# Moving waits off the small wait-carrying products, and reordering the attention work among the convolutions, in a one-core attention and convolution kernel

## What is computed

```python
q = einsum('bhwd,de->bhwe', x, Q_P)
k = einsum('bhwkd,de->bhwke', stk, K_P)      # stk: the nine shifted views, zero padded
v = einsum('bhwkd,de->bhwke', stk, V_P)
alpha = softmax(einsum('bhwke,bhwe->bhwk', k, q) * mask, axis=-1)
t = x + einsum('bhwk,bhwke->bhwe', alpha, v)
t_in = t
t = relu(conv3x3(t, ff1) + b1)
t = relu(conv3x3(t, ff2) + b2)
t = relu(conv3x3(t, ff3) + b3)
return t_in + t
```

## Time and profile before

| | |
|---|---|
| median of 3 runs | 2383.03 us (2382.46 to 2383.31) |
| the profiled execution's own time | 2380.99 us |
| its span, first to last instruction | 2379.0 us |
| TensorE busy | 96% |
| VectorE busy | 80% |
| ScalarE busy | 47% |
| DMA engines, mean share | 46.4% |
| mean granted TensorE clock | 0.993 |

### The profile page before, as it was taken

The page is one execution under the profiler, slowest core; times in us unless marked ns, Lnnn a source line. Parts: engine busy times, 40 slices in busy tenths (PEclk is TensorE's granted clock), DMA queues, the critical chain, the costliest instruction groups (busy, mean ns, idle before and its releaser), DMA issues.

```text
span 2379.0 us, 65460 instructions
## 1 busy us (share of the span) xinstructions
PE 2287.5 (96%) x25180; PEld 1317.7 (55%) x25180; DVE 1895.5 (80%) x2851; ACT 1127.4 (47%) x3108; POOL 15.5 (1%) x24
## 2 busy tenths in 40 slices
PE   4999999999999999999999999999998999999998
PEld 2655555555565555555555555555555555555554
DVE  4888888887588888888768888888877888888886
ACT  1554455444454554454345544544535445444543
POOL 2000000000000000000000000000000000000000
PEclk9999999999899999999999999999999999999999
DMA  4444544544355445444344454445434544454443
GB/s 125 138 137 136 158 134 125 160 141 134 94 158 152 137 126 162 139 136 137 123 138 144 126 160 140 135 136 157 135 124 119 156 147 138 127 160 136 128 153 119
DMA packets 291286, 328.79 MB, mean 138 GB/s; under 512 B 89300, under 2 KB 223252, under 8 KB 284564
## 3 DMA queue, kind: packets, MB, share of 16 engines
q1 hardware_dynamic: 291164, 327.17, 46.4%
HBM read 152.50 MB, written 33.82 MB: 78 GB/s over the span
## 4 chain that ended last, share of the span: by engine, by line
PE 79%; DVE 12%; issue 5%; ACT 1%; DVEq 1%; DMA 1%; SPq 0%; ACTq 0%
PE conv_banks L476 28%; PE conv_banks L435 16%; PE conv_banks L490 15%; PE mix_bank L413 6%; PE score_banks L387 3%; DVE work L836 3%; PE score_banks L398 3%; PE mix_bank L425 3%; DVE dt L764 2%; DVE tf L746 2%; DVE dt L760 2%; PE score_banks L381 1%; PE proj_bank L420 1%; PE score_banks L395 1%; PE conv_banks L450 1%
## 5 line engine op out<-in xcount | busy, mean ns | idle before, releaser
L476 PE MATMUL conv_banks<-dodd,w3f 128*64 128x512 f32 (+1 forms) x1656 | 500.3, 579 | 6.2 <-DVE dodd L760 3.9
L476 PE MATMUL conv_banks<-deven,w3f 128*64 128x512 f32 (+1 forms) x1656 | 489.9, 566 | 0.0
L598 ACT ACTIVATE prob<-score_banks,negmax 128x100 f32<-128x100 f32 x1040 | 343.0, 343 | 273.4 <-DVE negmax L726 273.4
L435 PE MATMUL conv_banks<-dt,w1f 128*64 128x256 f32 (+3 forms) x4224 | 414.4, 384 | 0.0
L490 PE MATMUL conv_banks<-duh,w2h 64*128 64x512 f32 (+2 forms) x1632 | 362.2, 423 | 4.0 <-ACT m_sb L634 2.1
L664 ACT ACTIVATE relued<-work,bias 128x1024 f32<-128x1024 f32 (+2 forms) x136 | 150.4, 1108 | 435.7 <-DVE work L836 435.7
L490 PE MATMUL conv_banks<-duh,w2l 64*128 64x512 f32 (+2 forms) x1632 | 329.5, 382 | 0.0
L435 PEld LDWEIGHTS conv_banks<-dt,w1f 128*64 128x64 f32 (+1 forms) x4224 | 219.2, 135 | 138.6 <-issue 65.9
L490 PE MATMUL conv_banks<-dul,w2h 64*128 64x512 f32 (+2 forms) x1632 | 286.4, 383 | 0.0
L476 PEld LDWEIGHTS conv_banks<-dodd,w3f 128*64 128x64 f32 x1656 | 138.8, 137 | 226.5 <-issue 181.3
L490 PEld LDWEIGHTS conv_banks<-duh,w2h 64*128 64x128 f32 x1632 | 168.7, 185 | 137.7 <-issue 104.5
(11 more groups left out here) (97 smaller groups left out, 3224.2 us busy)
## 6 DMA issues: line engine op xcount, KB each, us to landing
xk<-x_keys SPq DMA_DIRECT2D x66, 800.0 KB
xc<-x_bands SPq DMA_DIRECT2D x66, 650.0 KB, 5.0
dodd<-dodd SPq DMA_DIRECT2D x68, 512.0 KB, 5.1
xr<-x_bands SPq DMA_DIRECT2D x264, 128.0 KB, 3.5
out<-work SPq DMA_DIRECT2D x60, 512.0 KB, 2.7
dt<-dt SPq DMA_DIRECT2D x68, 256.0 KB, 2.3
deven<-deven SPq DMA_DIRECT2D x68, 256.0 KB, 5.7
duh<-duh SPq DMA_DIRECT2D x68, 256.0 KB, 2.4
```

The source lines that it names most:

```text
L435: mm = nc.tensor.matmul(bank[(LOWER, UPPER)[o], n * 256 + lo * 64:n * 256 + hi * 64], w1f[i][rows, m, s, o * C:o * C + C], dt[rows, lo + s ...
L476: return nc.tensor.matmul(bank[rows, lo * 128:hi * 128], w3f[:, m, s, odd * C:odd * C + C], source[:, lo + s // 2:hi + s // 2, m], start=s ...
L598: last = nc.scalar.activation(prob[:, g % 2, a], score_banks[:, g % 2, a * KEYS:(a + 1) * KEYS], ACT.Exp, bias=negmax[:, g % 2, a:a + 1], ...
```

## The change

On TensorE the small products are taken out of the loop. The waits that stood before them are functions of their own (`await_band`, `await_r`, `await_prob`, `await_y`), and are called inside the stream of products that comes before (`ahead`): before the last two products of a `conv3_tile`, before the last pair of `begin2` or `end2`, or inside the first `conv1` group. The waits of `conv1` itself stay where they are. Only in the prologue do the small products stay, as `hold`.

The third convolution's streams run in the order 0, 1, 2, 3 (before 0, 2, 1, 3). `begin2` takes both row taps against the high part of the data, and `go_on2` keeps only the low part; in the four streams together the products are the same. The first `mix` moves from between `go_on2` and `begin2` to behind the last `conv3_tile`; the second `turn` moves from behind `go_on2(1)` to between `begin2(1)` and `go_on2(1)`.

On ScalarE `keep_r(b, 0)` goes to the front, `keep_r(b, 1)` ahead of `keep_u2`, and `keep_m2(CONV3)` ahead of `relu_conv1`. On VectorE part 1 of `t_inputs` moves past the step's border, to behind `outer(ODD)`; `max_scores(b, 0)` goes ahead of `middle1`, and part 1 of the `inputs` of the second convolution's results goes behind `outer1`, between the two `scale`. SyncE's order of transfers is not changed.

```diff
-    return ORDER3.index(j) if which == CONV3 else 4 + 2 * j + (which == EVEN)
+    return j if which == CONV3 else 4 + 2 * j + (which == EVEN)
...
+            def hold(bank):
+                nc.tensor.matmul(bank[:, 0:2], eye16_sb[:], window_sb[:, 0:2], start=True, stop=True)
+            def await_band(b):
+                pe.wait_ge(t_ready, b * 2)
+                pe.wait_ge(xc_in, b * 16 + 16)
+                pe.wait_ge(xs_in, b * 32 + 32)
...
             def r_product(b):
-                if not isinstance(b, int):
-                    pe.wait_ge(t_ready, b * 2)
-                pe.wait_ge(xs_in, b * 32 + 32)
-                nc.tensor.matmul(proj_bank[:, 0:2], eye_sb[LOWER], eye_sb[LOWER, 0:2], start=True, stop=True)
...
+            def await_r(b, half):
+                pe.wait_ge(r_ready, b * 2 + (half + 1))
+                if half:
+                    pe.wait_ge(probt_ready, b * 2 + 1)
             def scores(b, half):
-                pe.wait_ge(r_ready, b * 2 + (half + 1))
-                if not isinstance(b, int) or half:
-                    pe.wait_ge(probt_ready, b * 2 + half)
-                nc.tensor.matmul(score_banks[:, 0, 0:2], eye16_sb[:], window_sb[:, 0:2], start=True, stop=True)
...
+            def await_prob(b, half):
+                pe.wait_ge(prob_ready, b * GROUPS + (2 * half + 2))
             def turn(b, half):
-                pe.wait_ge(prob_ready, b * GROUPS + (2 * half + 2))
-                nc.tensor.matmul(score_banks[:, 0, 0:2], eye_sb[LOWER], eye_sb[LOWER, 0:2], start=True, stop=True)
...
+            def await_y(b):
+                pe.wait_ge(y_ready, b * 2 + 2)
             def v_product(b):
-                pe.wait_ge(y_ready, b * 2 + 2)
-                pe.wait_ge(r_ready, b * 2 + 2)
-                nc.tensor.matmul(proj_bank[:, 0:2], eye_sb[LOWER], eye_sb[LOWER, 0:2], start=True, stop=True)
...
-            def conv1(G, k, b, outer):
+            def conv1(G, k, b, outer, att=False):
-                nc.tensor.matmul(conv_banks[:, 2 * outer, 0:2], eye16_sb[:], window_sb[:, 0:2], start=True, stop=True)
                 for n, m in enumerate(streams):
                     for i in range(2):
+                        if att and n == 1 and i == 1:
+                            await_r(b, 0)
...
 -            def conv3_tile(G, k, j):
+            def conv3_tile(G, k, j, ahead=None):
...
                 tap(1, 1, False, False)
+                if ahead:
+                    ahead()
                 tap(0, 1, False, True)
                 tap(1, 3, False, True).then_inc(tile_done, 1)
...
 -            def begin2(G, k, j):
+            def begin2(G, k, j, ahead=None):
...
-                for w in (w2h, w2l):
-                    tap2(k, EVEN, j, LOWER, 0, w, duh, w is w2h, False)
-                    tap2(k, ODD, j, UPPER, 0, w, duh, w is w2h, False)
+                for s in range(2):
+                    for w in (w2h, w2l):
+                        if ahead and s == 1 and w is w2l:
+                            ahead()
+                        tap2(k, EVEN, j, LOWER, s, w, duh, s == 0 and w is w2h, False)
+                        tap2(k, ODD, j, UPPER, s, w, duh, s == 0 and w is w2h, False)
             def go_on2(G, k, j):
-                for w in (w2h, w2l):
-                    tap2(k, EVEN, j, LOWER, 1, w, duh, False, False)
-                    tap2(k, ODD, j, UPPER, 1, w, duh, False, False)
...
 -            def end2(G, k, j):
+            def end2(G, k, j, ahead=None):
...
+                    if ahead and n == 2:
+                        ahead()
...
             def step(G, k, b, att):
                 if att:
-                    pe.wait_ge(xc_in, b * 16 + 16)
                     r_product(b)
-                conv1(G, k, b, False)
+                conv1(G, k, b, False, att)
                 if att:
                     scores(b, 0)
                 conv1(G, k, b, True)
                 conv3_tile(G, k, 0)
-                conv3_tile(G, k, 2)
+                conv3_tile(G, k, 1, (lambda: await_prob(b, 0)) if att else None)
                 if att:
                     turn(b, 0)
-                conv3_tile(G, k, 1)
+                conv3_tile(G, k, 2, (lambda: await_r(b, 1)) if att else None)
                 if att:
                     scores(b, 1)
                 conv3_tile(G, k, 3)
+                if att:
+                    mix(b, 0)
                 begin2(G, k, 0)
                 go_on2(G, k, 0)
-                if att:
-                    mix(b, 0)
-                begin2(G, k, 1)
+                begin2(G, k, 1, (lambda: await_prob(b, 1)) if att else None)
+                if att:
+                    turn(b, 1)
                 go_on2(G, k, 1)
-                if att:
-                    turn(b, 1)
...
-                begin2(G, k, 2)
+                begin2(G, k, 2, (lambda: await_y(b)) if att else None)
                 if att:
                     v_product(b)
...
-                end2(G, k, 3)
+                next_band = None if k == BANDS - 2 else b if k == BANDS - 1 else b + 1
+                end2(G, k, 3, None if next_band is None else lambda: await_band(next_band))
...
         @block.scalar
...
             def step(G, k, b, par, att):
+                if att:
+                    keep_r(b, 0)
                 if k:
                     relu_conv2(G, k - 1, ODD, 1)
-                if att:
-                    keep_r(b, 0)
-                if k:
                     relu_conv2(G, k - 1, EVEN, 1)
+                if att:
+                    keep_r(b, 1)
                 keep_u2(G, k)
                 if att:
                     exps(b, 0)
                     exps(b, 1)
-                    keep_r(b, 1)
+                keep_m2(G, k, CONV3)
                 relu_conv1(G, k)
-                keep_m2(G, k, CONV3)
...
         @block.vector
...
             def step(G, k, b, par, att):
                 if k:
                     outer(G, k - 1, ODD, 1)
+                if k < BANDS:
+                    t_inputs(None, b - 1, k % 2, 1)
+                if k:
                     outer(G, k - 1, EVEN, 1)
                     inputs(G, k - 1, ODD, 0, 1)
                     inputs(G, k - 1, EVEN, 0, 1)
+                if att:
+                    max_scores(b, 0)
                 middle1(G, k)
                 if att:
-                    max_scores(b, 0)
+                    max_scores(b, 1)
+                outer1(G, k)
+                if att:
+                    scale(b, 0)
+                if k:
+                    inputs(G, k - 1, EVEN, 1, 1)
+                if att:
+                    scale(b, 1)
                 if k:
                     inputs(G, k - 1, ODD, 1, 1)
-                if att:
-                    max_scores(b, 1)
-                if k:
-                    inputs(G, k - 1, EVEN, 1, 1)
-                outer1(G, k)
-                if att:
-                    scale(b, 0)
-                    scale(b, 1)
...
                     add_x(k, b, par, 1)
                     add_x(k, b, par, 0)
-                    for part in range(2):
-                        t_inputs(G, b, par, part)
+                    t_inputs(G, b, par, 0)
```

More of the change, by code:

```diff
@@ L532, in _ @@
             pe.wait_ge(xc_in, 16)
+            pe.wait_ge(xs_in, 32)
+            hold(proj_bank)
             r_product(0)
+            await_r(0, 0)
+            hold(score_banks[:, 0])
             scores(0, 0)
+            await_prob(0, 0)
+            hold(score_banks[:, 0])
             turn(0, 0)
+            await_r(0, 1)
+            hold(score_banks[:, 0])
             scores(0, 1)
             mix(0, 0)
+            await_prob(0, 1)
+            hold(score_banks[:, 0])
             turn(0, 1)
             mix(0, 1)
+            await_y(0)
+            hold(proj_bank)
             v_product(0)
@@ L589, in _ @@
                 step(g0 + BANDS, BANDS, b0 + BANDS, True)
-            for j in ORDER3:
+            for j in range(4):
                 conv3_tile(ALL_STEPS, 0, j)
@@ L688, in step @@
             def step(G, k, b, par, att):
-                if k:
-                    relu_conv2(G, k - 1, ODD, 1)
                 if att:
@@ L870, in _ @@
             dve.wait_ge(w_ready, 3)
-            for part in range(2):
-                t_inputs(None, 0, 0, part)
+            t_inputs(None, 0, 0, 0)
             def step(G, k, b, par, att):
@@ L891, in step @@
                     scale(b, 0)
+                if k:
+                    inputs(G, k - 1, EVEN, 1, 1)
+                if att:
                     scale(b, 1)
+                if k:
+                    inputs(G, k - 1, ODD, 1, 1)
                 inputs(G, k, CONV1, 0)
```

10 lines of the change are left out of this document (4 added, 6 removed).

## The result

The changed kernel takes 2293.84 us (median of 4 runs, 2291.31 to 2295.79) against 2383.14 for the kernel before: a ratio of 0.9625, 95% interval 0.9609 to 0.9642. That is 89.3 us less; 82.8 were forecast, a median of 2300. Its profiled execution takes 2292.98 us, 2291.0 of them the span.

The account below looks back on a forecast made before the run. TensorE's stream, busy 96% of the span, was taken as the bound. Terms 0.44 + 0 + 0.22 + 0.43 + 0.19 = 1.28 us a step, 82.8 in all, gave 2298.2, as a median 2300; range 2284 to 2316.

Parts of the forecast that it names:

- the first case: Whole kernel: all moved waits are met, 2300 us, own range 2284 to 2316; chance 0.63.
- The regular step: Steps k = 2 to 14, from one `r_product` to the next: 34.68 us before, 33.40 forecast.
- `conv1` and `scores`: Four bfloat16 small products dropped on TensorE: 0.11 us each, 0.44 a step; bounds nothing and 0.18 each.
- `r_product`: Its small product behind the last `end2` pair: worth nothing, wholly covered while `conv1` waits for `outer(ODD)`.
- `turn`: Two float32 small products on LOWER only: 0.11 us each, 0.22 a step; bounds nothing and 0.31.
- `v_product`: Small product and wait for ScalarE's copy after `begin2(2)`: 0.43 us saved, bounds 0.2 and 0.49; wait met with 0.05 spare.
- The mixing: First `mix` moved behind the third convolution: one leaving and one coming back saved, 0.19 us; bounds 0 and 0.3.
- The tightest place: VectorE's `middle1` ahead of the third convolution: done at 8.0 to 8.25 us, needed by 8.37, 0 to 0.25 spare.
- The rival that `middle1` comes late: Handing over before the third convolution costs 0.5 us more, each step gives back 0.5: 2332 us; chance 0.22.
- the forecast's own signs of being wrong: A gap before the third convolution, a stall inside `begin2` or a `conv3_tile`, or longer first products of a stream.
- The part of `t_inputs`: Part 1 left ahead of `outer(ODD)` on VectorE would make that about 0.5 us late; moved, it waits for nothing.
- The rival by the floor: Skill's 25 ns floor: four small products worth 0.10 us, step gain about 0.6, near 2345; no chance of its own.

Follow-up runs that it names:

- the version with the masks in the gap: Changed kernel with the four mask products of the first `scores` moved between `r_product` and the inner `conv1`: 2282.88 us, ratio 0.9580.
- the version after it: Changed kernel with the mask products between `r_product` and inner `conv1`, and `middle1` ahead of the first `max_scores` in steps k = 0, 1 and 16: 2279.64 us.

## Why the prediction was right, point by point

**The total.** Right: 2300 forecast, 2293.8 measured, inside the first case's own range of 2284 to 2316. Two errors of opposite sign lie in it. The regular step was to be 33.40 and is 33.06; 52 of them give 1.62 x 52 = 84 us where 1.28 x 52 = 67 were counted. The twelve short steps with attention and the four without were to give 16; they and the prologue give about 4, the rest of the span's 88.0. So there is luck in the total: with the step's true 1.62 in all 64 steps, the forecast's own reckoning ends at 2381.0 - 103.7 - 0.9 + 2.0 = 2278, outside its range. That range isn't the sum of the bounds either: with the lower ones of the turns (0), the mixing (0) and the V product (0.2) together, 0.64 a step, it would have reached up to 2341.

**The short steps.** Measured from the first product of the inner `conv1` to the next one's: k = 0 is shorter by 0.9 us on average, k = 1 by 0.40 (30.98 to 30.58), k = 15 longer by 0.06 (28.22 to 28.28), and the four k = 16, the last of them to the span's end, are longer by 3.5 in all. The prologue gives 1.8 (`conv1` starts at 50.40 against 52.20). A step k = 16 takes 33.52 where the clock doesn't fall behind the wait for `middle1`, against 33.42 and 33.64 before (35.87 in the first pair); 35.20 where it falls; 37.92 in the third pair, where the turn of the loop behind it takes 6.64 us without work instead of 3.9 as well.

**`conv1` and `scores`.** Terms of 0.11 each. Shown for `conv1` and for the second `scores`; in the first `scores` 0.23, since the 128 x 128 product stood between two streams of 64 x 64 products and brought a change of shape (from the inner `conv1`'s first product to the outer one's it took 4.11 and takes 3.77, and 0.11 of the 0.34 are the outer `conv1`'s own). Mis-sized by 0.12: 0.56 for the four where 0.44 was forecast.

**`r_product`.** Costed at nothing. Shown twice: with its product put back, and with four masks more in the gap, the start of `conv1` stays at 1.81.

**`turn`.** 0.22 for two, measured 0.80 - 0.58 = 0.22 for the first (0.80 from 740.38 to 741.18 in the experiment that puts it back), and 0.17 for the second (from the turn to the second mixing 753.73 - 751.10 = 2.63 in that experiment, 728.20 - 725.74 = 2.46 without), so 0.39. The row of `r_product`'s small product, of the same kind, has 0.20 to the next start (1380.49 to 1380.69) and would have been the nearer one.

**`v_product`.** 0.43 forecast; 0.34 measured. The copy is waited for a little still: the last pair takes 0.39 where a pair and the way out take 0.33 (701.57 to 701.90). The mechanism is the one written down, 0.05 to spare turned into about 0.06 short.

**The mixing.** 0.19 forecast, 0.33 measured by putting it back: the way out of the third convolution (0.1) was missing from the term, and the mixing itself is shorter there by 0.04.

**The tightest place.** `middle1` was named as such, with 0 to 0.25 to spare; in the regular step it has about 0.15 when the handing over is counted. The order that the forecast redid holds there: `scale` 1 ended at 12.20 and part 1 of ODD at 13.34 us into the step (12.2 and 13.3 forecast). The rival that `middle1` comes late is true in the steps k = 16, whose short first convolution gives it less cover, and for 0.20 us in k = 15. There the forecast was too simple: it gave every step with attention the regular step's gain, said of `r_product` in k = 0 and k = 1 that these steps "can only add to the gain", and didn't look at k = 16. In k = 16 TensorE waited 2.08 us, and in three of the four the clock fell behind the wait. In k = 0 and k = 1 the probabilities are late in the second tile (0.31 and 1.44 us). Both are among the forecast's own signs of being wrong; they came in the short steps alone.

**The orders of ScalarE and VectorE.** The forecast used the new orders' times without saying what they are worth. Put back beside the new order of the tiles, they cost 1.1 us a step, as much as the small products. So dropping the products and moving the waits would have given little without them; how much of the 1.1 hangs on the order of the tiles wasn't measured (0.7 us would stay by the estimate above). The part of `t_inputs` gives 0.47, forecast 0.5.

**The rival by the floor.** Putting the small products back cost 1.04 us a step, 0.15 for each of the seven that count; the forecast, which went by the row of 0.11, was near and still too low. The Trainium skill, *TensorE: Matmul & The Clock Gate*, section "Back-to-back issue gap", would put the seven, three of them with two records, at 10 x 0.025 = 0.25 us, an estimate. The section calls the figure a floor, which 1.04 doesn't contradict; as a price for these products it is too low by a factor of four.

## What to carry to other kernels

Price a small product by the distance of starts around it, and count the changes of shape on both sides of it, not its record. Find the gaps in which an engine waits anyway before removing work in them: nothing is won there, and independent work fits in for free. A wait moved forward into a stream must be met by the other engines' order in every form of the step; recompute it for the shortest one, and reorder the other engines together with it. Look too at the waits that tiles carry themselves: reordering the tiles moves them.

## What the runs showed of the hardware

A product pair of the third convolution (128 rows, 64 columns) is followed by one of `mix` (100 rows, 64 columns) at its usual 0.43 us, but by products of 64 x 64, 64 x 100 or 64 x 128 only at 0.53. Between the last 64 x 64 products of `conv1` and the masks (float32 to bfloat16, the same shape) no time shows as lost. In the other places a change between shapes costs about 0.1 us on the way out and about as much on the way back in (0.34 for the first pair of the second convolution, 0.235 for the others).

Within 1.1 us of the end of the wait of 2.08 us in the steps k = 16, the granted clock went to 0.50 for 3.4 us in three of the four steps, and the products there took up to twice their time. It costs 1.7 us: 35.20 against 33.52 for two such steps that are otherwise alike. The wait alone doesn't decide it: with 2.24 us, in the version with the masks in the gap, it fell in one of four, and with 1.76, in the version after it, in one of four too. What decides stays open. Whether it is why the four runs of the changed kernel lie 4.5 us apart isn't shown: their mean granted clocks (0.987 at 2292.98, 0.992 at 2295.79 and 2294.70, 0.993 at 2291.31) don't order them.

Where the loop over the pairs of images turns, TensorE stands without anything that the profile shows it waiting for: 3.39, 3.55 and 3.77 us in the kernel before, 3.94, 3.93 and 6.64 in the changed one. At the turns of the inner loop no such time shows.
